# VectorE adds o ahead of weighting the scores in pass 1; the first sigmoids and the last transposition of x2n stand earlier in pass 2

## The reference

```python
mod = (silu(c) @ wmod).reshape(6, 512)          # sa, ca, ga, sb, cb, gb; |ga|, |gb| at least 0.25
h = layernorm(x) * (1 + ca) + sa
q, k, v = h @ Wq.T, (h @ Wk.T) * sigmoid(h @ Wg.T), h @ Wv.T     # 16 heads of 64
g = -softplus(h @ Wd.T + bd)                                     # one log decay per token and head
s_t = exp(g_t) * s_(t-1) + k_t^T v_t;   o_t = q_t s_t            # over all tokens
o = o * rsqrt(mean(o * o) + eps) * norm_w * sigmoid(h @ Wog.T)
x = x + ga * (o @ Wo.T)
h = layernorm(x) * (1 + cb) + sb
xr = mu_r * h + (1 - mu_r) * previous(h);   xk = mu_k * h + (1 - mu_k) * previous(h)
x = x + gb * sigmoid(xr @ W_r.T) * (relu(xk @ W_k.T)^2 @ W_v.T)
```

## Time and profile before

| | |
|---|---|
| median of three runs | 3260.14 us |
| profiled execution | 3259.97 us |
| its span, first to last instruction | 3258.0 us |
| mean granted TensorE clock | 0.989 |
| TensorE (PE) busy | 3171.0 us, 97% |
| VectorE (DVE) busy | 1878.4 us, 58% |
| ScalarE (ACT) busy | 1294.3 us, 40% |
| GpSimd (POOL) busy | 471.9 us, 14% |
| DMA, mean | 86 GB/s |

### The profile page before, as it was taken

How to read it: one execution, slowest core, us unless ns; L and a number is a source line. 1 busy time by engine, 2 the same in 40 slices (tenths; PEclk the granted TensorE clock), 3 DMA queues, 4 the chain that set the end, 5 groups by cost and what they waited for, 6 DMA issues and landing times. The chain is left out here.

```text
span 3258.0 us, 96723 instructions
## 1 busy us (share of the span) xinstructions
PE 3171.0 (97%) x37253; PEld 2972.0 (91%) x37253; DVE 1878.4 (58%) x4825; ACT 1294.3 (40%) x3584; POOL 471.9 (14%) x723
## 2 busy tenths in 40 slices
PE   7999999999999999999999969999999999999998
PEld 6999999999999999999999968999999999999997
DVE  5454554545545545455454555766666767777776
ACT  3444444444444444444444443333333333333332
POOL 0111111111111111111111111111111111111110
PEclk8999999999999999999999989999999999999999
DMA  6132222322223222232222243232222333322220
GB/s 214 58 103 73 88 90 68 104 68 89 89 69 106 67 90 89 68 105 67 93 86 72 89 142 92 81 81 83 77 77 77 82 86 83 82 79 77 77 77 27
DMA packets 273330, 278.93 MB, mean 86 GB/s; under 512 B 24720, under 2 KB 221344, under 8 KB 273072
## 3 DMA queue, kind: packets, MB, share of 16 engines
q1 hardware_dynamic: 270960, 270.67, 27.4%
q10 hardware_dynamic: 2112, 4.19, 0.4%
HBM read 189.84 MB, written 84.93 MB: 84 GB/s over the span
## 5 line engine op out<-in xcount | busy, mean ns | idle before, releaser
L55 PE MATMUL psJ<-h_hi,w_g_hi 128*128 128x256 f32 x1024 | 295.7, 289 | 14.6 <-ACT q L770 11.9
L55 PE MATMUL psJ<-h_hi,w_k_hi 128*128 128x256 f32 x1024 | 298.9, 292 | 0.0
L55 PE MATMUL psJ<-h_hi,w_q_hi 128*128 128x256 f32 x1024 | 296.7, 290 | 1.9 <-issue 1.2
L55 PE MATMUL psG<-h_hi,w_og_hi 128*128 128x256 f32 x1024 | 287.7, 281 | 7.4 <-PEq L348 4.1
L56 PE MATMUL psJ<-h_lo,w_q_hi 128*128 128x256 f32 x1024 | 286.8, 280 | 0.1
L57 PE MATMUL psJ<-h_hi,w_q_lo 128*128 128x256 f32 x1024 | 286.4, 280 | 0.2 <-issue 0.2
L57 PE MATMUL psJ<-h_hi,w_g_lo 128*128 128x256 f32 x1024 | 286.6, 280 | 0.0
L56 PE MATMUL psJ<-h_lo,w_g_hi 128*128 128x256 f32 x1024 | 286.5, 280 | 0.0
L57 PE MATMUL psJ<-h_hi,w_k_lo 128*128 128x256 f32 x1024 | 285.3, 279 | 0.0
L56 PE MATMUL psJ<-h_lo,w_k_hi 128*128 128x256 f32 x1024 | 285.2, 279 | 0.0
L56 PE MATMUL psG<-h_lo,w_og_hi 128*128 128x256 f32 x1024 | 284.9, 278 | 0.0
(11 more groups left out here) (238 smaller groups left out, 9309.2 us busy)
## 6 DMA issues: line engine op xcount, KB each, us to landing
grown<-cum_dram SPq DMA_DIRECT2D x256, 128.0 KB
cum_rows<-cum_dram SPq DMA_DIRECT2D x512, 64.0 KB, 3.6
o_dram<-o SPq DMA_DIRECT2D x256, 128.0 KB, 3.6
o_cols<-o_dram SPq DMA_DIRECT2D x128, 256.0 KB, 4.9
an_norm_x<-in_L_attn_x_dram SPq DMA_DIRECT2D x32, 512.0 KB, 4.8
h_dram<-h_hi SPq DMA_DIRECT2D x32, 512.0 KB, 2.7
h_dram<-h_lo SPq DMA_DIRECT2D x32, 512.0 KB, 3.8
h_hi<-h_dram SPq DMA_DIRECT2D x32, 512.0 KB, 4.0
```

Of the source, the lines that this page charges most:

```text
L55: nc.tensor.matmul(out, w_hi, x_hi, start=first, stop=False)
```

## The change

In VectorE's program for pass 1, `sum_o` stands ahead of `weigh_scores`; in step 0, where it adds the last pairs of the tile before, it stands ahead of `gate_k` as well. In pass 2 tile 0 has its first two sigmoids (with the load of ScalarE's table) ahead of the squares. The last tile's x2n is made as soon as its statistics are there and turned after the products with W_r of tile 30, ahead of those with W_k, instead of after all products of tile 30. The mixer's part of the last tile has programs of its own (`pe_end`, `dve_end`): its r takes other buffers (z_hi and z_lo for the mixed rows, psW for the product, o_cols for the sigmoid, psG and psT for the products with W_k), so that it need not wait for those of tile 30, and its result is added to x1 directly, without the copy to x1_old. The loops of pass 2 hold the same instructions in the same order as before.

```diff
--- before.py
+++ after.py
@@ -1041,13 +1041,15 @@
                     gate_k(dve, i, 2 * d - 1)
                 grow_q(dve, j, d)
                 grow_state(dve, j, d)
+                if d == 0 and not opens:
+                    sum_o(dve, j - 1, ND - 1)
                 if proj:
                     gate_k(dve, i, 2 * d)
                 if proj and d == 3:
                     keep_rows(dve, i)
+                if d > 0:
+                    sum_o(dve, j, d - 1)
                 weigh_scores(dve, j, d)
-                if d > 0 or not opens:
-                    sum_o(dve, j if d else j - 1, (d - 1) % ND)
                 if prep > 1 and d == 2:
                     norm_stats(dve, i + 2)
...
+        psK_end = psG + [psT[:, 0, :], psT[:, 2, :]]
+        r_end = o[:, 0:KD, :].rearrange("p (c k) t -> p c (k t)", c=NC)
+        rows_end = (z_hi[:, 0:KD, :], z_lo[:, 0:KD, :])
+        acts_end = (z_hi[:, KD:NP, :], z_lo[:, KD:NP, :])
...
+        def pe_end(pe, j):
+            pe.wait_ge(s["xr"], j + 1)
+            pe.wait_ge(s["relu"], KD * j)
+            for c in range(NC):
+                rows_product(psW[c], *rows_end, W["r"], c, 0, KD).then_inc(s["rr"], 1)
+            pe.wait_ge(s["xk"], j + 1)
+            pe.wait_ge(s["h2"], KD * (j + 1))
+            for n in range(KD):
+                for k in range(KD):
+                    wh, wl = (a[:, k, n * P:(n + 1) * P] for a in W["k2"])
+                    last = three_passes(nc, psK_end[n][:, 0:T], wh, wl, xk_hi[:, k, :], xk_lo[:, k, :], k == 0,
+                                        k == KD - 1)
+                last.then_inc(s["kt"], 1)
+            pe.wait_ge(s["fin1"], NC * j)
+            for c in range(NC):
+                ready = [(k, pe, s["ka"], KD * j + k + 1) for k in range(KD)]
+                rows_product(psR[c], *acts_end, W["v2"], c, 0, KD, ready if c == 0 else ()).then_inc(s["kv"], 1)
...
+            if att and not prep:
+                turn_x2(pe, i)
...
+            def open_gate(n):
+                act.wait_ge(s["og"], 4 * i + n + 1)
+                hold(act, s["z"], 4 * i + n - 1)
+                nc.scalar.activation(og[:, n % 2, :, :], psG[n % 2][:, :].rearrange("p (b t) -> p b t", b=2),
+                                     ACT.Sigmoid).then_inc(s["sg"], 1)
+
+            def affine_h2(m):
+                hold(act, s["last"], m + 1)
+                for k in range(KD):
+                    act.wait_ge(s["xT2"], KD * m + 2 * (k // 2) + 2)
+                    nc.scalar.activation(h2[:, k, 1:T + 1], psT[:, k, :], ACT.Identity, bias=t["mod"][:, SB, k:k + 1],
+                                         scale=t["cb1"][:, k:k + 1]).then_inc(s["h2"], 1)
+
             if att:
+                if not ffn:
+                    for n in range(2):
+                        open_gate(n)
...
                 for n in range(4):
-                    act.wait_ge(s["og"], 4 * i + n + 1)
-                    hold(act, s["z"], 4 * i + n - 1)
-                    nc.scalar.activation(og[:, n % 2, :, :], psG[n % 2][:, :].rearrange("p (b t) -> p b t", b=2),
-                                         ACT.Sigmoid).then_inc(s["sg"], 1)
+                    if ffn or n > 1:
+                        open_gate(n)
...
-                hold(act, s["store"], 16 * NC * j)
+                if att:
+                    hold(act, s["store"], 16 * NC * j)
+                else:
+                    act.wait_ge(s["zl"], 4 * NT)
                 for c in range(NC):
                     act.wait_ge(s["rr"], NC * j + c + 1)
-                    nc.scalar.activation(r[:, c, :], psR[c][:, :], ACT.Sigmoid).then_inc(s["rs"], 1)
+                    gates, product = (r, psR) if att else (r_end, psW)
+                    nc.scalar.activation(gates[:, c, :], product[c][:, :], ACT.Sigmoid).then_inc(s["rs"], 1)
+            if att and not prep:
+                affine_h2(i)
...
+        def dve_end(dve, j):
+            dve.wait_ge(s["h2"], KD * (j + 1))
+            shift(0, s["prev"])
+            dve.wait_ge(s["rr"], NC * j)
+            for n in range(KD):
+                split_act(dve, j - 1, n, ra_hi, ra_lo)
+            mix_shifted(dve, j, 0, *rows_end, s["prev"], s["mixr"], s["xr_hi"], s["xr"])
+            dve.wait_ge(s["kt"], KD * j)
+            dve.wait_ge(s["xr"], j + 1)
+            shift_mix(dve, j, 1, xk_hi, xk_lo, s["prevk"], s["mixk"], s["xk_hi"], s["xk"])
+            for c in range(NC):
+                add_out(dve, j - 1, c, r, x1_old)
+            for n in range(KD):
+                split_act(dve, j, n, *acts_end)
+            dve.wait_ge(s["rs"], NC * (j + 1))
+            dve.wait_ge(s["store"], 16 * NC * j)
+            for c in range(NC):
+                add_out(dve, j, c, r_end, x1)
...
+            if att and not prep:
+                norm_second(dve, i)
+                return
```

More of the change, by code:

```diff
@@ L1296, in _ @@
             pe_tile(pe, NT - 1, True, True, False)
-            pe_tile(pe, NT, False, True, False)
+            pe_end(pe, NT - 1)
         def act_tile(act, i, att, ffn, prep):
@@ L1322, in act_tile @@
                 copy_z(3)
+            if att and ffn:
+                affine_h2(j)
             if ffn:
[L1324 to L1329, removed]
-                hold(act, s["store"], 16 * NC * j)
+                if att:
+                    hold(act, s["store"], 16 * NC * j)
+                else:
+                    act.wait_ge(s["zl"], 4 * NT)
                 for c in range(NC):
                     act.wait_ge(s["rr"], NC * j + c + 1)
-                    nc.scalar.activation(r[:, c, :], psR[c][:, :], ACT.Sigmoid).then_inc(s["rs"], 1)
+                    gates, product = (r, psR) if att else (r_end, psW)
+                    nc.scalar.activation(gates[:, c, :], product[c][:, :], ACT.Sigmoid).then_inc(s["rs"], 1)
+            if att and not prep:
+                affine_h2(i)
             if ffn:
@@ L1377, in shift_mix, with mix_shifted @@
             last.then_inc(s_prev, 1)
+        def mix_shifted(dve, j, m, hi, lo, s_prev, s_mix, s_hi, s_lo):
             dve.wait_ge(s_prev, j + 1)
@@ L1387, in shift_mix, with split_act, add_out @@
             nc.vector.tensor_tensor(lo[:, :, :], mix[:, :, :], hi[:, :, :].bitcast(F32), ALU.subtract).then_inc(s_lo, 1)
+        def shift_mix(dve, j, m, hi, lo, s_prev, s_mix, s_hi, s_lo):
+            shift(m, s_prev)
+            mix_shifted(dve, j, m, hi, lo, s_prev, s_mix, s_hi, s_lo)
+        def split_act(dve, j, n, hi, lo):
+            dve.wait_ge(s["k2"], KD * j + n + 1)
+            nc.vector.tensor_copy(hi[:, n, :], relu[:, n % 2, 1, :]).then_inc(s["ka_hi"], 1)
+            dve.wait_ge(s["ka_hi"], KD * j + n + 1)
+            nc.vector.tensor_tensor(lo[:, n, :], relu[:, n % 2, 1, :], hi[:, n, :].bitcast(F32),
+                                    ALU.subtract).then_inc(s["ka"], 1)
+        def add_out(dve, j, c, gates, base):
+            dve.wait_ge(s["kv"], NC * j + c + 1)
+            nc.vector.tensor_tensor(r[:, c, :], psR[c][:, :], gates[:, c, :], ALU.mult).then_inc(s["fin1"], 1)
+            dve.wait_ge(s["fin1"], NC * j + c + 1)
+            nc.vector.tensor_tensor(r[:, c, :], base[:, c, :], r[:, c, :], ALU.add).then_inc(s["fin"], 1)
+        def dve_end(dve, j):
[16 more added lines that the diff above has]
+                add_out(dve, j, c, r_end, x1)
         def rest_z(dve, i, n):
@@ L1428, in dve_tile @@
                 for n in range(KD):
-                    dve.wait_ge(s["k2"], KD * j + n + 1)
-                    nc.vector.tensor_copy(ra_hi[:, n, :], relu[:, n % 2, 1, :]).then_inc(s["ka_hi"], 1)
-                    dve.wait_ge(s["ka_hi"], KD * j + n + 1)
-                    nc.vector.tensor_tensor(ra_lo[:, n, :], relu[:, n % 2, 1, :], ra_hi[:, n, :].bitcast(F32),
-                                            ALU.subtract).then_inc(s["ka"], 1)
+                    split_act(dve, j, n, ra_hi, ra_lo)
             if att:
@@ L1455, in _ @@
             dve_tile(dve, NT - 1, True, True, False)
-            dve_tile(dve, NT, False, True, False)
+            dve_end(dve, NT - 1)
         def rsqrt(pool, which, n, ready, done):
```

10 lines of the change are left out of this document (4 added, 6 removed).

## The result

The changed kernel took 3238.62 us (median of four runs, 3233.84 to 3240.09), the kernel before on the same chip 3260.98 us (four runs): ratio 0.9927, 95% interval 0.9915 to 0.994, 22.4 us less. Forecast were 3237.7 us and 22.3 us less. The profiled execution after is the quickest of the four, 3233.84 us with a span of 3231.8 us.

| stretch | before | after | gained | forecast |
|---|---|---|---|---|
| start to the first h_lo of tile 2 | 166.35 | 165.45 | 0.9 | – |
| from there to the first h_lo of tile 31 (29 tiles) | 1680.08 | 1666.04 | 14.0 | 12 |
| to the first matmul of pass 2 | 118.44 | 116.62 | 1.8 | 2.4 |
| to the sums of squares of pass 2's second tile | 42.36 | 39.34 | 3.0 | 1.1 |
| to the second sigmoid of r, tile 30 | 1209.00 | 1209.47 | -0.5 | 0 |

A forecast was written before the change was run, and what follows sets the result against it. TensorE was taken as the bound, its waits falling in four places: 12 + 2.4 + 1.1 + 6.8 = 22.3 us off 3259.97 us gives 3237.7 us (3230 to 3246 by its bounds; range 3229 to 3251 us).

The forecast's parts named there:

- The four places: Tiles of pass 1, its last tile, head and tail of pass 2: 12, 2.4, 1.1 and 6.8 us, together 22.3 us.
- Tiles of pass 1: The sum moved at d = 3 starts SyncE's stores sooner, so TensorE waits less for q: 12 us, bounds 0 and 18.2.
- the store's landing follows its issue, 0.65 us: Pass 1: the store of o goes out 0.65 us sooner with SyncE's chain, and its landing moves with it.
- rival B: Pass 1: the store lands no sooner, its landing set by queued traffic, not its issue; 3250.3 us, chance 0.15.
- The count of tiles that pay: Pass 1: 15 recorded TensorE waits plus three ScalarE waits above 1.9 us, so 18 x 0.65 = 11.7 us.
- Last tile: End of pass 1: chain starts 0.65 us sooner and three sums fall into VectorE's idle time: 2.4 us, bounds 0.6 and 3.5.
- Head: Start of pass 2: a 2.4 us wait for sums of squares replaces one of 3.33 us; 1.1 us gained, bounds 0 and 3.
- Tail: End of pass 2: 6.52 us wait and 2.45 us of slow clock go, 2.2 us wait comes; 6.8 us, bounds 5 and 7.5.
- The slack of 0.3 us in VectorE's chain: Tail of pass 2: VectorE's mix, hi and lo end 0.3 us before TensorE asks for them.
- C: Tail of pass 2: VectorE's chain comes late and the clock falls, 5 to 7 us lost; about 3244 us, chance 0.07.
- D: Pass 1, d = 0: the sum ahead of the gate of k delays TensorE, making the kernel slower; 3283 us, chance 0.03.
- E: Pass 1: all TensorE's waits for q go, 24.5 us gained instead of 12; 3225 us, chance 0.05.

The follow-up runs named there:

- stores_first: Kernel before, only SyncE's queue changed: at d = 0 stores of pairs 6 and 7 go ahead of the copies of cum's rows; 3245.66 us, ratio 0.995.
- cum_first: Kernel before, only SyncE issues the two stores of cum's rows ahead of the stores of pairs 4 and 5 at d = 3; 3236.62 us, ratio 0.9927.
- h_later: Kernel before, only SyncE's stores of h moved from the start of d = 0 to the end of d = 1; 3243.28 us, ratio 0.9944.
- experiment 2: Pass 1's swaps split, against the kernel before: only the one at d = 3, 3247.03 us; only those at d = 0, 1 and 2, 3259.65 us.
- experiment 5: Two kernels from the changed one: GpSimd's first sums of squares held back behind VectorE's gating and split of o, 3227.92 us; last x2n turned later, 3233.16 us.
- pass2_only: Kernel before with only the change's pass 2 part, pass 1 as before; 3255.25 us, ratio 0.9982.
- mid_turn: Changed kernel with the last x2n turned behind two of the four products with k2 of the tile before, not ahead of all four; 3233.16 us, one execution.
- all_but_d3: Kernel before with pass 1's swaps at d = 0, 1 and 2 but not the one at d = 3; 3259.65 us, ratio 0.9997.
- after_stores_first: Changed kernel with SyncE issuing the stores of pairs 6 and 7 ahead of the copies of cum's rows at d = 0; 3234.29 us, ratio 0.9915.

## Why the prediction was right, and where it was not

*The sum.* 22.3 us were forecast, 22.4 us measured by the medians. The four places and what moves in each were right; that the totals agree within 0.1 us is luck. The places as the traces have them add up to some 25 us (15.1 + 2.3 + 1.2 + 6.5), 3 us more than the medians; one term was too small by 3 us, and the head and tail of a given execution vary by some 5 us with the clock.

*Tiles of pass 1: 12 us forecast, 15 us measured.* Over four traces with all swaps (1666.04, 1665.50, 1665.07, 1663.22 us) and two without (1680.08, 1680.06 us) the gain is 15.1 us. The step "the store's landing follows its issue, 0.65 us" is the one that was off, with a small effect. The store went out 0.76 us sooner and landed 0.97 us sooner in the mean (15.27 instead of 16.24 us behind h_lo), h at the head of its burst went out 0.94 us sooner. And the landing does not follow the store's own issue, as stores_first shows (3.3 us of it moved the landing by 0.8 us); it follows the chain as a whole. Which transfer in the chain sets it stays open: with h in the burst the landing comes 12.0 us behind h's issue (before, the changed kernel and cum_first), but without h it is hardly quicker (h_later). I had seen the 1 MB of h in rival B and used it against the gain, as if a landing set by traffic could not move; the traffic moves with the chain. That SyncE's wait for the sum at d = 3 starts the chain was right and is shown by the runs of experiment 2 and by cum_first. The count of tiles that pay was good enough: ScalarE's waits fell by 27.2 us in the profiled execution and TensorE got back 14.0.

*Last tile: 2.4 us forecast, 1.8 in the profile.* Over five traces with all swaps it took 116.4 us in the mean, over four with neither a swap nor cum_first's order 118.7: 2.3 us. In VectorE's timeline after, the sums stand in the idle time and only the second score waits:

```profile
1918.53 0.75 DVE L951 TENSOR_TENSOR o<-o,psP 128x256 f32<-128x256 f32 x2
...
1921.69 0.42 DVE L974 TENSOR_TENSOR prob<-prob,psB 128x256 f32<-128x256 f32 x1 [2.08 <-ACT prob L802]
```

*Head: 1.1 us forecast, 3.0 in the profile, 1.2 over four traces.* The new wait is 2.9 us, not 2.4: the sums ended 5.8 us behind the squares instead of 5.26, and the contention seen in experiment 5 accounts for it. That I let the clock fall after this pause was right in pass2_only and mid_turn, wrong in the profiled execution; and the 1.6 us that I took for the fall is too little, it cost 2.8 us. That the term comes out at 1.2 us is the mean of two traces with the fall (0.2 and -0.7 us) and two without (3.0 and 2.4 us), so its agreement is luck too. ScalarE's order came out as forecast, the table's 1.28 us followed at once by the sigmoid:

```profile
1952.79 1.28 ACT L1336 ACT_TABLE_LOAD   x1 [8.07 <-PE psG L57]
1954.08 0.60 ACT L1336 ACTIVATE og<-psG 128x512 f32<-128x512 f32 x1
```

*Tail: 6.8 us forecast, 6.9 measured;* 5.3 us in pass2_only, whose clock fell, near the lower bound of 5. The mean of four traces with this tail is 31.4 us, of seven with the old one 37.9 us. The slack of 0.3 us in VectorE's chain was counted too small: in mid_turn the turn is later by about 2 us and TensorE still doesn't wait for it.

*Rivals.* B falls as a forecast, by the tiles' gain; its thought that the landing is not set by the store's own issue holds. C did not happen; its condition, a fallen clock, did in one trace and cost 1.6 us. D falls with all_but_d3. E did not come: the tiles gained 15.1 us and 4 of 15 waits for q stayed. It takes cum_first to remove them, for 20.5 us.

## What to carry to other kernels

A wait of the bounding engine may begin with another engine's order of two instructions, some 30 us and a whole queue of DMA issues ahead: follow it back to what the queue stood waiting for, and first try to reorder the queue itself, which here (cum's rows ahead of o's stores) gave in one exchange what the whole change gave. A DMA's landing is to be measured against everything issued in its burst, not only its own issue: where another transfer moves with it, both hypotheses fit, and only a run that moves one alone tells them apart (h_later was meant as that run, and moved the store as well). A gain that hangs on a pause of 2 to 3 us of TensorE should be given as a range, from more than one trace.

## What the runs showed of the hardware

- After pauses of one length TensorE's granted clock fell in some executions and not in others: 2.9 us, at 1.00 behind it in the changed kernel and in after_stores_first, 0.50 in pass2_only and mid_turn, which cost 2.8 us; 2.1 us, 1.00 in the changed kernel, 0.70 to 0.73 over six microseconds in pass2_only.
- A store of 128 KB landed 12.0 us behind the issue of 1 MB ahead of it in the same queue, although h's own stores land in 2.7 to 5.5 us. Issued 3.3 us sooner it landed 0.8 us sooner (7.3 instead of 4.8 us to its landing). With the 1 MB taken out it still took 4.5 us to land, 9.6 us behind the issue of two copies of 128 KB (grown). What holds it no run here shows.
- VectorE and GpSimd working at once in SBUF: two gatings that take 1.29 us together took 3.50 us beside a sum of GpSimd's, which itself took 2.90 instead of 2.39 us. I had named the rule and let it cost nothing; it is the 0.5 us by which the new wait was longer.
